# Router logits computed transposed, three edge steps brought forward, the expert bias added by a product, and two unread products behind each routed tile's transposes

## The reference

```python
xn  = layernorm(x)
h   = tanh(mean_over_edges(xn) @ W1_l.T + xn @ W1_r.T + b1)          # two graph layers
gnn = mean_over_edges(h) @ W2_l.T + h @ W2_r.T + b2
q, k, v = split(xn @ w_qkv)                                          # linear attention, 8 heads
mix = (phi(q) @ (phi(k).T @ v) / (phi(q) . sum(phi(k)))) @ w_proj + b_proj
x   = x + gnn + mix
xf  = layernorm(x)
logits = xf @ Wr + br                                                # 8 experts, the best one of each node
e   = argmax(logits);  gate = softmax(of that one logit)             # = 1
x   = x + gate * (relu(xf @ W1[e] + b1[e]) @ W2[e] + b2[e])
```

## Time and profile before

| | us |
|---|---|
| median of 3 runs (2669.18 to 2678.6) | 2670.3 |
| the profiled execution | 2669.17 |
| its span, first to last instruction | 2667.3 |
| PE busy | 2505.4 |
| DVE busy | 1780.9 |
| POOL busy | 1190.3 |
| ACT busy | 1106.4 |
| mean granted TensorE clock | 0.929 |

### The profile page before, as it was taken

How to read it: one execution, slowest core, us unless ns; L and a number is a source line. 1 busy time by engine, 2 the same in 40 slices (tenths; PEclk the granted TensorE clock), 3 DMA queues, 4 the chain that set the end, 5 groups by cost and what they waited for, 6 DMA issues and landing times.

```text
span 2667.3 us, 39329 instructions
## 1 busy us (share of the span) xinstructions
PE 2505.4 (94%) x11432; PEld 2037.1 (76%) x11433; DVE 1780.9 (67%) x3721; ACT 1106.4 (41%) x2035; POOL 1190.3 (45%) x1092
## 2 busy tenths in 40 slices
PE   5999999999999998999999799999999599969997
PEld 4788888888888886888888577777677499967675
DVE  5577777867777854344444388888888466647887
ACT  3445544444444443434444233333333144425554
POOL 5677767666666650000000055555555345432333
PEclk8999999999999998999999899999999755559999
DMA  9867666554555544544444478877787676636554
GB/s 372 253 172 203 169 189 167 124 158 120 148 142 124 157 91 181 222 190 189 176 177 168 171 202 236 241 229 220 220 239 215 175 313 258 246 122 190 182 180 139
DMA packets 159530, 511.57 MB, mean 192 GB/s; under 512 B 30483, under 2 KB 30995, under 8 KB 126787
## 3 DMA queue, kind: packets, MB, share of 16 engines
q1 hardware_dynamic: 110148, 381.72, 40.2%
q0 software_dynamic: 49280, 128.61, 21.5%
HBM read 268.07 MB, written 244.32 MB: 192 GB/s over the span
## 4 chain that ended last, share of the span: by engine, by line
PE 73%; DMA 14%; DVE 4%; issue 4%; POOL 2%; ACT 1%; SPq 1%; DVEq 0%; POOLq 0%; ACTq 0%
PE bank L1348 46%; DMA agg_d<-O,eidx 11%; PE bank L1399 8%; PE bank L1355 6%; PE bank L1590 3%; PE bank L1533 2%; PE bank L1463 1%; PE bank L1593 1%; PE bank L450 1%; PE bank L451 1%; POOL r_rows L796 1%; PE bank L1551 1%; DMA a_x<-in_x 1%; PE bank L1579 1%; PE bank L1581 1%
## 5 line engine op out<-in xcount | busy, mean ns | idle before, releaser
L411 POOL DMA_INDIRECT agg_d<-O,eidx x160 | 276.5, 1728 | 247.6 <-DMA agg_d<-O,eidx 197.0
L347 POOL TENSOR_TENSOR G_low<-G,G_high 128x512 fp32r<-128x512 f32 x160 | 243.4, 1521 | 194.5 <-ACT G_high L472 194.2
L394 POOL DMA_INDIRECT G<-y_d,esrc x80 | 85.4, 1067 | 529.2 <-DMA y_d<-b_y 516.8
L430 DVE SCALAR_TENSOR_TENSOR Sj<-erow,dstf,tri 128x128 f32<-128x128 int32 x160 | 182.3, 1139 | 48.0 <-DMA agg_d<-O,eidx 48.0
L472 ACT CAST G_high<-G 128x512 fp32r<-128x512 f32 x160 | 99.2, 620 | 195.4 <-DVE G L1060 166.1
L807 POOL DMA_INDIRECT out<-x_out,x_id x88 | 84.4, 959 | 188.9 <-DVE x_out L1303 182.7
L439 DVE SCALAR_TENSOR_TENSOR eidx<-cnt,todump,dstf 128x1 int32<-128x1 f32 x160 | 161.7, 1011 | 7.6
L1533 PEld LDWEIGHTS bank<-wr,r_xnT 128*128 128x128 f32 x640 | 142.9, 332 | 5.7 <-issue 4.5
L1533 PE MATMUL bank<-wr,r_xnT 128*128 128x8 f32 x640 | 142.8, 357 | 0.0
L761 POOL TENSOR_TENSOR pd<-pd,low 128x512 f32<-128x512 f32 (+1 forms) x80 | 142.1, 1777 | 0.0
L347 POOL TENSOR_TENSOR a_xn_rows_low<-a_x,a_xn_rows_high 128x512 fp32r<-128x512 f32 x80 | 141.7, 1771 | 0.3 <-ACT a_xn_rows_high L833 0.3
(11 more groups left out here) (225 smaller groups left out, 7664.8 us busy)
## 6 DMA issues: line engine op xcount, KB each, us to landing
x_rows<-xs_d SPq DMA_DIRECT2D x88, 260.0 KB
agg_d<-zero SPq DMA_DIRECT2D x20, 1040.0 KB, 20.1
b_agg<-agg_d SPq DMA_DIRECT2D x20, 1040.0 KB, 8.8
a_x<-in_x SPq DMA_DIRECT2D x20, 1024.0 KB
agg_d<-z_halves SPq DMA_DIRECT2D x20, 1024.0 KB
q_d<-q_rows SPq DMA_DIRECT2D x80, 256.0 KB
r_d<-r_rows SPq DMA_DIRECT2D x80, 256.0 KB
r_in<-r_d SPq DMA_DIRECT2D x20, 1024.0 KB, 6.8
```

Source lines behind the costliest of these rows:

```text
L347: return eng.tensor_tensor(out_, full, high.bitcast(F32), ALU.subtract)
L394: pool.indirect_dma_start(G[:, j, :], None, table, bass.IndirectOffsetOnAxis(ap=esrc[:, b, j:j + 1], axis=0)).then_inc(e_g[j], 16)
L411: pool.indirect_dma_start(agg, bass.IndirectOffsetOnAxis(ap=eidx[:, j, 0:1], axis=0), O[:, j, 0:width], None, compute_op=ALU.add).then_inc ...
L430: dve.scalar_tensor_tensor(Sj[:, :], row, dstf[:, b, j:j + 1], tri[:, :], ALU.is_equal, ALU.mult, accum_out=cnt[:, j:j + 1]).then_inc(e_cn ...
```

## The change

Five edits.

1. **Turned routing products.** `logits` makes the router weights (8 columns) the stationary operand and the transposed tile (128 columns) the moving one; the result is 8 x 128 for each tile. ACT copies the 8 x 512 result of a group to `lgT` and adds the bias `br` as a bias per partition; at the head of its next turn PE turns it back with four transposes of 8 x 128 (`turn_logits`), and DVE reads the logits from PSUM. DVE's addition of `brs` goes.
2. **Two unread products.** Behind each tile's four transposes PE issues two float32r matmuls of 512 columns into a bank that nobody reads.
3. **Doubled edge steps.** Two edge steps instead of one go with steps 12, 20 and 28 of the mix stage; edge steps run 3 behind, and the tail is 8 steps.
4. **Early partial sums.** SP loads the parts of groups 0 to 3 and issues the last two stores of the mix stage before it waits for the last edge scatter; behind the wait stand the four aggregates.
5. **Bias by a product.** In the expert stage the biases lie split in `b1s` on partitions 0 (high) and 32 (low), and one matmul of 64 columns on 33 rows adds them into PSUM; DVE's L1309 becomes an ACT copy.

Semaphores of the fold and of the biases are merged so that the new ones have room.

```diff
-            now = 0 if t < 6 else 1
+            now = 0 if t < 6 else 1 + (t in (12, 20, 28))
...
+            def part_in(g, k):
+                sp.dma_start(rp[k][:, :, :].rearrange("p j n -> p (j n)"), part_d[g]).then_inc(r_in[k], 16)
+            def agg_in(g, k):
+                sp.dma_start(ra[k][:, :, :].rearrange("p j n -> p (j n)"), agg2_g[g]).then_inc(r_in[k], 16)
             sp.wait_ge(m_st[0], 16 * (PAIRS - 1))
             sp.wait_ge(m_qz, NT)
-            sp.dma_start(rp[0][:, :, :]..., part_d[0]).then_inc(r_in[0], 16)
+            part_in(0, 0)
+            mix(PAIRS, 5)
+            mix(PAIRS + 1, 1)
+            sp.wait_ge(m_p, NT)
+            part_in(3, 3)
+            sp.wait_ge(m_st[0], 16 * PAIRS)
+            part_in(1, 1)
+            sp.wait_ge(m_st[1], 16 * PAIRS)
+            part_in(2, 2)
             sp.wait_ge(e_sc, 16 * 2 * NT)
-            sp.dma_start(ra[0][:, :, :]..., agg2_g[0]).then_inc(r_in[0], 16)
-            mix(PAIRS, 5)
-            sp.wait_ge(m_p, NT)
-            sp.dma_start(ra[1][:, :, :]..., agg2_g[1]).then_inc(r_in[1], 16)
-            mix(PAIRS + 1, 1)
-            sp.wait_ge(m_st[0], 16 * PAIRS)
-            sp.dma_start(rp[1][:, :, :]..., part_d[1]).then_inc(r_in[1], 16)
-            sp.wait_ge(m_st[1], 16 * PAIRS)
+            for k in range(4):
+                agg_in(k, k)
...
-            turns(pool, mix, 11, head=4, last=1)
+            turns(pool, mix, 8, head=4, last=1)
...
@@ ACT, end of a routing turn @@
+                    act.wait_ge(r_l, 4 * g)
+                    need(act, r_l2, g - 2)
+                    act.activation(lgT[0:EXP, 1 - k % 2, :], bank[3 - k % 2][0:EXP, :], ACT.Identity,
+                                   bias=brc[0:EXP, 0:1]).then_inc(r_lt, 1)
@@ ACT, expert step @@
+                if active(s, 4, XT):
+                    act.wait_ge(x_h, s - 3)
+                    act.copy(xt1[:, b, :], bank[2 + b][:, EH:P]).then_inc(x_t1, 1)
...
@@ DVE, best() @@
-                    dve.wait_ge(r_l, 4 * (g - 1))
-                    dve.tensor_tensor(lg[:, :, :], bank[...], each(brs), ALU.add).then_inc(r_ch, 1)
+                    dve.wait_ge(r_l2, g - 1)
...
@@ DVE, expert step @@
-                    e = dve.value_load(tabE[0:1, bass.ds(16 * turn4 + k4, 1)], min_val=0, max_val=EXP - 1)
-                    dve.wait_ge(x_h, s - 3)
-                    dve.tensor_tensor(xt1[:, b, :], bank[2 + b][:, EH:P], b1s[:, bass.ds(e, 1), :]..., ALU.add)
                     need(dve, x_ht, s - 5)
+                    dve.wait_ge(x_t1, s - 3)
...
@@ PE, routing @@
-                        last = pe.matmul(bank[2 + 4 * ((k - 1) % 2)][:, col:col + EXP], rxT[:, j % 2, c, :], wrs[:, c, :], ...)
+                        last = pe.matmul(bank[3 - k % 2][0:EXP, j * P:(j + 1) * P], wrs[:, c, :], rxT[:, j % 2, c, :], ...)
+                def turn_logits():
+                    need_apart(pe, r_lt, g - 1)
+                    need_apart(pe, r_ch, CH * (g - 4) + 3)
+                    for j in range(TG):
+                        last = pe.transpose(bank[4 + k % 2][:, EXP * j:EXP * (j + 1)],
+                                            lgT[0:EXP, k % 2, j * P:(j + 1) * P], ident[0:EXP, 0:EXP])
+                    last.then_inc(r_l2, 1)
                 def turn_row(j):
                     turn_tile(bank[j % 2], rxn[:, j % 2, :]).then_inc(r_tr, 1)
+                    for e in range(2):
+                        pe.matmul(bank[7][:, :], allp[0:HD, :], W2b[0:HD, e, :], start=True, stop=True)
+                if active(g, 2, NG):
+                    turn_logits()
...
@@ PE, expert step @@
+                    pe.matmul(bank[3 - b][:, 0:EH], allp[0:LOW + 1, :],
+                              b1s[0:LOW + 1, bass.ds(e, 1), :].rearrange("p a h -> p (a h)"),
+                              start=False, stop=False)
```

More of the change, by code:

```diff
@@ L204, in build @@
         cst = word("moe_constants", 0, [CW])
[L205 to L206 removed]
+        wrs = word("wr", 256, [KC, EXP])
+        b1s = word("b1_halves", 312, [EXP, EH], F32R)
+        brc, rev, first = word("br", 288, [1]), cst[:, 296:304], cst[:, 304:312]
         order, idn = cst[:, 824:824 + XT], cst[:, 1040:1040 + NT]
         before, allp = word("r_before", 1120, [P], F32R), word("r_all", 912, [P], F32R)
[L209 to L210 removed]
+        eq, sc, onehot, pos = (word(f"r_{n}", 1280 + 32 * i, [TG, EXP], F32R if i == 2 else F32) for i, n in
+                               enumerate(("equal", "score", "onehot", "place")))
+        lgT = at("r_logitsT", 9.125, shape=[P, 2, GROUP])
         mx, td, te, rt, m2, pf = (word(f"r_{n}", 1408 + 8 * i, [TG]) for i, n in
@@ L949, in mix @@
                     act.copy(b2s[0:EXP, :], b2raw[0:EXP, :]).then_inc(s_b2, 1)
+                if isinstance(t, int) and t == 24:
+                    act.wait_ge(s_craw, 16 * 8)
+                    act.copy(b1s[0:HD, :, :].rearrange("p e h -> p (e h)"), b1raw[0:HD, :]).then_inc(s_b2, 1)
             act.wait_ge(b_yst[1], 16 * (PAIRS - 1))
@@ L954, in _ @@
                     mix(0, k)
-            turns(act, mix, 11, head=4, last=1, skip=5)
+            turns(act, mix, 8, head=4, last=1, skip=5)
             def route(turn, k):
@@ L1178, in mix @@
                     low_half(dve, b2s[LOW:STACK, :], b2raw[LOW:STACK, :], b2s[LOW:STACK, :]).then_inc(s_b2, 1)
-            turns(dve, mix, 11, head=4, last=1)
+                if isinstance(t, int) and t == 25:
+                    dve.wait_ge(s_b2, 4)
+                    b1low = b1s[LOW:HD, :, :].rearrange("p e h -> p (e h)")
+                    low_half(dve, b1low, b1raw[LOW:HD, :], b1low).then_inc(s_b2, 1)
+            turns(dve, mix, 9, head=4, last=1)
             dve.wait_ge(s_craw, 16 * 8)
@@ L1516, in mix @@
                     edge_pe(pe, 1, *te, bank[7][:, :])
-            turns(pe, mix, 11, head=4, last=1, skip=6)
+            turns(pe, mix, 8, head=4, last=1, skip=6)
             pe.wait_ge(s_craw, 16 * 8)
+            pe.wait_ge(s_b2, 5)
             pe.wait_ge(m_qz, NT)
```

95 lines of the change are left out of this document (40 added, 55 removed).

## The result

| | before | after |
|---|---|---|
| median of the runs, us | 2669.74 (2666.42 to 2678.6) | 2729.32 (2728.75 to 2735.69) |
| ratio after / before, 95% interval | | 1.0228 (1.0212 to 1.0245) |
| span of the profiled execution | 2667.3 | 2727.0 |
| mean granted clock (1.00 is full speed) | 0.929 | 0.958 |
| mean routing turn, us | 12.64 | 13.91 |

What follows compares the result with a forecast made beforehand. Routing was taken as held by PE's work at half clock, within 7.17 of a 12.54 us turn. Terms: 2669.2 - 30 + 8 + 4 - 11 - 5 + 1 = 2,636 us; range 2,604 to 2,668, without A and B's far end.

Steps and rivals of the forecast that it cites:

- 1.82 + 1.82 + 0.83 us of streamed columns: Routing: gapless streaming in a cold turn, expected to raise the clock in the first or second PE turn.
- Rival A: Routing: the clock stays down, PE sets a 17.4 us turn, 19 x 4.9 = +93, 2,747 us; chance 0.13.
- Rival B: Routing: the clock falls in every turn, which costs 12.5 us as before; 2,655 us; chance 0.15.
- Two of the signs that I had set for being wrong: Signs set: PEclk 5 in routing; PE gaps at mix steps 12, 20, 28; turn above 12 us at high clock.
- That is 1.6 to 1.7 less a turn; I take 1.6, 19 turns, -30 us: Routing at full clock: ACT's start to places falls from 7.17 to 5.5 us, the turn to 10.9.
- A tile's pair is 0.43 warm: Routing: two unread 512-column products cost 0.43 us at full clock, 0.83 cold; three pairs on the path.
- the other engines allow that: Routing turn of 10.9 us: DVE has 8.1 us a group, the DMA engines 8.3, PE 8.5.
- Falls of the clock, +8: Routing: a fall about every fourth turn, five of them at 1.7 us each, +8 us.
- Doubled steps and early parts, -11: Entry to routing: first x2 near 2,108, 8 us sooner, and group 1 3.5 us more; bounds -4 and -16.
- Rival C: Mix stage: each doubled step costs its full 5.6 us and the entry gains nothing; 2,653 us; chance 0.08.
- Bias by a product, -5: Expert stage: 0.08 us saved a step over 88 steps, -7; at worst +8; taken as -5 us.
- DVE's hidden rows gate PE: Expert step: PE's next L1590 waits for DVE's L1314 through PSUM bank reuse; without L1309 rows come 0.25 us sooner.

Runs made afterwards that it cites:

- The early scatter: POOL issues the first of a group's four row scatters before the scales, against turned products with six unread products at turn's end: 2631.08 us, 0.9872 of before.
- the six products at the turn's end: Six unread 512-column products on 128 rows at the end of PE's turn, against turned products only: 2652.91 us, 0.9939 of before.

## Why the prediction was wrong, point by point

*That the clock would rise and mostly hold* was right: 0.83 in the turns of after. The rise came where I had it, in the first or second PE turn. With the turned products alone PE starts at 2128.39, is busy 5.00 of 5.00 us at 0.50 from 2,129 to 2,134, and the clock is at 1.00 from 2134.4 on, in the first turn. In after PE is busy 14.90 of 14.90 us at 0.50 from 2132.6 to 2147.5, and the clock is first at 1.00 from 2149.5 to 2,152, in the second. So my 1.82 + 1.82 + 0.83 us of streamed columns were no measure of when it comes; what decides it is not shown. *Rival A, that it stays down*, came out on the same side as the result by another road; its mechanism is refuted by the clock. That its cold turn of 17.4 us is near the 17.31 of the kernel with the pairs only is luck: that kernel has neither turned products nor turning back, and the same terms give 16.2 for it. *Rival B* saw part of it: in after tile 0's products and tile 2's transposes run at half clock in 13 of 19 turns. Two of the signs that I had set for being wrong came: gaps on PE around steps 12, 20 and 28 of the mix stage, and a turn above 12 us at a high clock.

*"That is 1.6 to 1.7 less a turn; I take 1.6, 19 turns, -30 us"* is the first step that failed. Two terms of that turn were right: a turned product 0.107 to 0.11 us warm and 0.213 cold (forecast 0.113 and 0.227), rank products 1.0 (forecast 0.95). Two things were not. *"A tile's pair is 0.43 warm"*: with 64-row loads it is 0.66 us from its start to that of the next transposes, whose own start is late too, 1.25 for 0.87 together, and three of them are on the path; and behind the pairs the clock fell, which with 128-row pairs it didn't in the turn shown. Together 44 us. (Put on the kernel before alone, where the clock stays down, they cost 91.) And the turn without pairs had a floor that I had dismissed with *"the other engines allow that"*: I had compared sums of busy time (DVE 8.1 us a group), and POOL's chain, scales, then four scatters 1.27 us apart, then 1.8 us until places, closes at 11.4 us. So the turned products gave 11 us alone, where my chain (7.17 down to 4.2 without pairs) would have given 3 us a turn. The early scatter shows the rest: with it the chain is 4.7 us.

*Falls of the clock, +8*: a fall in every fourth turn was my estimate, from no row. In after 13 of 19 turns are partly cold, where I had five and the first. What such falls are worth without pairs is about 6 us, by the six products at the turn's end (0.81 to 0.92).

*Doubled steps and early parts, -11*: zero. Rival C was the right mechanism and had 0.08. I charged 2 us; PE lost 12 in the stretch that holds steps 12, 20 and 28. The last scatter did come 1.1 us sooner (2103.86 instead of 2104.94), but the last product came 12.7 later, and the first x2 at 2122.52 where I had 2,108.

*Bias by a product, -5*: 25 to 29 us the other way from no product, in three comparisons (1.0228 to 1.0131; 1.0065 to 0.9956; 0.9927 to 0.9835). The step that failed is *"DVE's hidden rows gate PE"*. The chain said "issue" there, and DVE's row ended 0.30 us ahead of the product; that two things end near one another was taken for one gating the other. The bound *"at worst PE's +0.09 alone, +8"* was from a product with a 128-row load, and it broke too: the product with its neighbours costs 0.31.

So the sum of the measured terms is: turned products -11, pairs +44, bias +26, the others 0: +59, of 60. The first was measured on the kernel before and the other two on after, and the intervals of each are several us wide, so the close agreement is in part luck.

The load of the stationary operand itself takes 0.18 us with 33 rows, 0.19 with 64 and 0.19 with 128 (in after); what differs is what stands around it. With 64 rows the unread pair and its transposes take 1.25 us, with 128 rows 0.96 (there the pair streams another operand as well); with 33 rows the bias product takes 0.22, with 128 rows 0.03. In the records of after (the step at 2,603 us) the load of 33 rows begins 0.33 us after the start of the 512-column product before it, and the full load behind it 0.22 us after the bias product's start, while full loads among the 512-column products begin within 0.01 us of the previous product's start; a 66-row load (L1612) overlaps too, it begins 0.09 us after the start of the product before it (2604.92 and 2604.83). Which number of rows is the border, and why, stays open.

## What to carry to other kernels

Price a small matmul by a row with the same number of stationary rows beside the same neighbours, and when it is 33 or 64 rows between full ones, try it with zeros up to 128 first; here pairs and bias product on 128 rows took 50 us off. When an edit makes one engine's part of a turn shorter, follow every other engine's chain of waits around the turn, not its busy time: the next bound here was a row of four scatters, which closes a turn at 11.4 us where I had forecast 10.9. Look for the cause of a gap that the chain calls "issue" in the engine's own order and instruction stream first; here two reads of a number and the addresses worked out from it cost 0.35 us a step. Why a bias product on 128 rows still lengthened the step by 0.18 us was not tested apart from its dynamic address.

## What the runs showed of the hardware that I had not expected

Float32 products with 8 stationary and 128 moving columns lifted the clock of routing from 0.50 to 0.81 with no other edit, while eight float32r products of 512 columns in each turn of a PE busy all the time left it at 0.50 (17.31 us a turn). A `places` on DVE whose inputs had been ready for 1.2 us started 1.77 to 1.89 us after POOL's fourth scatter had started, in nine turns of one kernel. And PE, the busiest engine at 94%, was held up by its own reads of a number and the addresses made from it: without them the expert step fell from 2.82 to 2.47 us and the kernel by 33 us.
